# Two edits in a graph network kernel: where VectorE prepares the next pair of tiles, and which engine adds an output bias

## The chip, the cores and the metric

The kernel runs on 1 core of one Trainium2 chip. The metric is device time in microseconds (us) for the whole program; lower is better.

## What the reference computes

The input is a graph of 12,500 nodes with 256 features each and 212,500 weighted edges. Everything is fp32.

```python
xn = _layernorm(x)
x = x + L0_gnn(xn, edges) + L0_mix(xn)       # layer 0: graph convolution, linear attention mixer
x = x + L0_ffn(_layernorm(x))                # layer 0: mixture of 8 experts, two best per token
xn = _layernorm(x)
x = x + L1_gnn(xn, edges) + L1_mix(xn)       # layer 1: graph sum, linear attention block
x = x + L1_ffn(_layernorm(x))                # layer 1: attention over slices

# inside L0_gnn
h = agg + (dinv * dinv)[:, None] * (xn @ W)  # the node's own share beside the sum over its edges
h = 0.5 * _layernorm(h + b) * gamma + ... + 0.5 * xn ; h = relu(h)

# inside L1_ffn, its last line: slice_weights is (12500, 512), slice_out is (512, 256)
return out_x @ W_out + b_out
```

The output is `x` after both layers, 12,500 x 256.

## The kernel before, in words

The program is a sequence of stages. Two of them are touched.

**`finish_layer0`** (span 3143 to 5930 us of the profile) takes what an earlier stage has summed over the edges (`k.sums`, kept in SBUF) and does the rest of layer 0: the product of the graph convolution, the query side of the mixer, the eight experts, and the key side of layer 1's norm. It works on *pairs* of tiles of 125 nodes, `TE` = 2 and `NP` = 50 pairs. Three pairs are in flight at once in one `run(i, n, turn)`: the experts of pair `i` (`moe`), the front of pair `f = i + 1` (`front`) and the back of pair `b = i - 1` (`back`). Each engine has its own copy of `run` with 32 *slots*, written out by hand; the order of the slots is the order of that engine's instructions, and semaphores couple the engines. TensorE issues in slot 0 and 1 the first layer ("up") of expert 0, in slot 2 and 3 the up products of expert 1, then down products and up products in turn (`chunk(slot)`), down products of expert 6 in slots 28 and 29, of expert 7 in slots 30 and 31. Slots 26 and 27 hold only up products of expert 7, so VectorE has no `expert_sum` there.

The pairs run as: two written-out runs (a prologue without experts, and run 0), then a hardware loop `Fori(0, (NP - 2) // 2)` with two runs in its body (runs 1 to 48), then two written-out runs. All engines share this `pipeline`.

What concerns the change, in the order of VectorE's slots:

- slot 0: `back_norm` (L1500, L1504: statistics of the experts' result `acc` of pair b), then four steps of `inverse_root`, then `x_and_sums(0)`; slot 1: four more steps, `x_and_sums(1)`; slot 2: the last four steps; slot 3: `back_rows` (L1562).
- `x_and_sums(j)` (L1570 to L1582): one `tensor_scalar` writes the normalised rows `xn` of pair f (L1576), one `scalar_tensor_tensor` writes `s = xn * dinv + sums` (L1580). It waits for the load of x (`x_in`), for the previous pair's residual chain (`h_chain`), and for the previous transposes (`T_done`).
- slot 4: `expert_sum(0, 0)` (L1543) and `gcn(0)` (L1587), which frees TensorE's PSUM bank `ps_M` for the query product.
- slot 13: `gcn_residual`, the last reader of `xn` and of `x` of pair f; SyncE then loads the x of the next pair (L1425).
- slots 24 and 25: `expert_sum` of expert 5; slot 28: `expert_sum(6, 0)`, then the router's logits (L1673).

TensorE transposes `xn` and `s` of pair f in slots 2 and 3 (`turn_xs`, L1947 and L1948, waits for `xs_ready`), ScalarE copies them out of PSUM (L1799), and TensorE multiplies them in slots 4 to 7 (`gcn`, `query`, both through L1953). TensorE's second-bias product (L1937) of slot 23 waits for VectorE's L1550.

**`write_out`** (span 9330 to 9634 us, the last stage) computes for 50 pairs of tiles x3 + slice weights @ `slice_out` + `b_out`. Per pair SyncE loads the slice weights `sw` and the rows `x3` into one of four buffers, TensorE turns `sw` with 8 transposes (L3120), ScalarE and VectorE copy one tile each out of PSUM (`keep`, L3093), TensorE forms the product of the pair before in `ps_o` (`product`, L3124 to L3131), VectorE adds `x3` to it (L3106), and GpSimd issues the stores (L3084). The product begins with one matmul of a row of ones by the bias (L3125, `start=True`), and 8 matmuls by `slice_out` (L3129) accumulate on top. A matmul of the program shows as two matmuls in the trace.

## Time and profile before

| | us |
|---|---|
| median of 3 runs | 9634.83 (9633.47 to 9641.52) |
| profiled execution, its own time | 9635.69 |
| span of the profiled execution, first to last instruction | 9634.1 |
| TensorE busy | 7447.9 (77%) |
| VectorE busy | 6285.8 (65%) |
| GpSimd busy | 5605.1 (58%) |
| ScalarE busy | 1679.3 (17%) |

The stages follow one another and have different limits, so these shares are only an average. `finish_layer0` fills about 29% of the span and `write_out` about 3%. The time outside the span is 1.6 us.

### The profile page before, as it was taken

What the parts mean: (1) busy time and instruction counts of PE and PEld (TensorE: products, weight loads), DVE (VectorE), ACT (ScalarE), POOL (GpSimd) and SP (SyncE); (2) the same over time, 40 slices, a digit from 0 to 9 for tenths busy, and PEclk for the clock granted to TensorE, in tenths of its full rate; (3) what the DMA queues carried; (4) which work ended last, traced back from release to release, by engine and by line L of the source; (5) the groups of instructions that cost most, each with busy time, mean ns of one, the idle gap of its engine ahead of it and who ended that gap; (6) DMA issues with size and microseconds to landing.
All of it is one profiled execution on the core that took longest, in us unless ns stands there. A gap on an engine that the chain in (4) does not pass through costs nothing. (4 is left out here: it accounts for less than half of the span.)

```text
span 9634.1 us, 141965 instructions
## 1 busy us (share of the span) xinstructions
PE 7447.9 (77%) x34023; PEld 5485.8 (57%) x34023; DVE 6285.8 (65%) x21621; ACT 1679.3 (17%) x3225; POOL 5605.1 (58%) x6034
## 2 busy tenths in 40 slices
PE   4834777677676788888888887788888888877779
PEld 3633555555555566666666665556555565655556
DVE  5746777777777666666666665566666666667742
ACT  0000000000000333433433432111111011112210
POOL 3225777777776555655655655777777777730002
PEclk7657888888888899999999997898898898889989
DMA  1024333333333100000000000333333333333336
GB/s 50 30 74 125 109 107 109 109 107 109 106 110 103 33 16 17 16 15 17 16 16 17 17 15 25 113 107 104 105 105 103 107 104 104 105 86 92 94 96 167
DMA packets 464055, 737.23 MB, mean 77 GB/s; under 512 B 145169, under 2 KB 317487, under 8 KB 463067
## 3 DMA queue, kind: packets, MB, share of 16 engines
q0 software_dynamic: 235408, 493.09, 18.3%
q1 hardware_dynamic: 214944, 224.70, 8.3%
q10 hardware_dynamic: 13240, 15.44, 0.6%
q14 instruction: 437, 3.58, 0.1%
q8 instruction: 26, 0.43, 0.0%
HBM read 624.32 MB, written 108.50 MB: 76 GB/s over the span
## 5 line engine op out<-in xcount | busy, mean ns | idle before, releaser
L894 POOL DMA_INDIRECT sum_gathered<-table,sum_idx x3600 | 3506.2, 974 | 1196.3 <-issue 996.4
L959 PE MATMUL sum_agg_res<-sum_gathered,sum_lay 125*125 125x256 f32 x7200 | 2259.6, 453 | 931.1 <-DMA sum_gathered<-table,sum_idx 346.5
L1463 POOL DMA_INDIRECT sorted_recs<-fin_rec,fin_pos x1700 | 1659.7, 976 | 1147.7 <-PE fin_ps_up L1916 656.8
L959 PEld LDWEIGHTS sum_agg_res<-sum_gathered,sum_lay 125*125 125x125 f32 x7200 | 1466.2, 218 | 1492.2 <-DVE all_sums L944 943.4
L944 DVE TENSOR_TENSOR all_sums<-all_sums,sum_agg_res 125x256 f32 x3600 | 1509.6, 419 | 1050.2 <-PE sum_agg_res L959 842.8
L925 DVE TENSOR_SCALAR sum_lay<-all_lane,sum_dloc_now,sum_w_now 125x125 f32<-125x125 f32 x3612 | 1281.0, 355 | 21.0 <-DVE sum_xn_tiles L1076 16.9
L1916 PE MATMUL fin_ps_up<-fin_tokens_T,fin_w 128*128 128x250 f32 x3200 | 865.2, 397 | 51.4 <-ACT fin_hidden L1791 51.4
L1924 PE MATMUL fin_ps_dn<-fin_w,fin_hidden 128*125 128x256 f32 x3200 | 883.7, 413 | 0.1
L1543 DVE SCALAR_TENSOR_TENSOR fin_acc<-fin_ps_dn,fin_comb,fin_acc 125x256 f32<-125x256 f32 x800 | 386.3, 483 | 562.0 <-PE fin_ps_dn L1924 553.4
L1916 PEld LDWEIGHTS fin_ps_up<-fin_tokens_T,fin_w 128*128 128x128 f32 x3200 | 600.3, 201 | 169.4 <-ACT fin_hidden L1791 86.6
L1924 PEld LDWEIGHTS fin_ps_dn<-fin_w,fin_hidden 128*125 128x125 f32 x3200 | 619.5, 204 | 130.0 <-issue 42.1
L1791 ACT ACTIVATE fin_hidden<-fin_ps_up,fin_b 128x250 f32<-128x250 f32 x800 | 370.4, 469 | 960.4 <-PE fin_ps_up L1916 958.6
L2462 PE MATMUL sum_ps_A<-sum_w,sum_low 128*125 128x256 f32 x1600 | 378.0, 379 | 0.0
L2710 POOL TENSOR_SCALAR slices_var_eps<-slices_mean_var 125x2 f32<-125x2 f32 x50 | 11.0, 219 | 616.2 <-DVE slices_mean_var L2753 604.0
L2453 PE MATMUL sum_ps_C<-sum_x_T,sum_w 128*128 128x500 f32 x800 | 368.4, 582 | 0.0
L2462 PEld LDWEIGHTS sum_ps_A<-sum_w,sum_low 128*125 128x125 f32 x1600 | 300.2, 188 | 116.0 <-issue 80.7
L1059 DVE CUSTOM_DVE_ANT_0 sum_junk<-sum_src_hot,sum_ps_rank 125x100 f32<-125x100 bf16 x1700 | 335.2, 253 | 1.5 <-PE sum_ps_rank L1127 1.5
L2827 PE MATMUL slices_ps_acc<-slices_xn,slices_sw 125*128 125x257 f32 x800 | 229.9, 439 | 121.3 <-DVE slices_sw L2778 121.3
L1049 DVE TENSOR_TENSOR sum_src_hot<-sum_lane,steps_src_tile 125x400 bf16<-125x400 bf16 x425 | 242.9, 571 | 65.6 <-PE sum_ps_rank L1135 58.9
L2385 ACT ACTIVATE sum_low<-sum_ps_C,sum_b 128x500 f32<-128x500 f32 x200 | 135.4, 677 | 722.0 <-PE sum_ps_C L2453 722.0
L1111 ACT ACTIVATE sum_exp_key<-sum_key_less_max 125x256 f32<-125x256 f32 x100 | 41.6, 416 | 1259.2 <-DVE sum_key_less_max L1086 1259.2
L2827 PEld LDWEIGHTS slices_ps_acc<-slices_xn,slices_sw 125*128 125x128 f32 x800 | 165.8, 218 | 166.8 <-DVE slices_sw L2778 142.4
(484 smaller groups left out, 10795.8 us busy)
## 6 DMA issues: line engine op xcount, KB each, us to landing
sum_gathered<-table,sum_idx POOLq DMA_INDIRECT x3600
sorted_recs<-fin_rec,fin_pos POOLq DMA_INDIRECT x1700
slice_weights<-slices_sw SPq DMA_DIRECT2D x50, 480.0 KB
out_sw<-slice_weights SPq DMA_DIRECT2D x50, 480.0 KB
deg_x_tiles<-in_x SPq DMA_DIRECT2D x100, 125.0 KB
sum_x_tiles<-in_x SPq DMA_DIRECT2D x100, 125.0 KB
fin_x<-in_x SPq DMA_DIRECT2D x100, 125.0 KB
x<-fin_acc SPq DMA_DIRECT2D x100, 125.0 KB
```

The lines of the kernel that those rows point to most:

```text
L894: eng.indirect_dma_start(out=self.rows[:, s % self.RING, :], out_offset=None, in_=self.table, in_offset=bass.IndirectOffsetOnAxis(ap=self. ...
L925: ins = eng.tensor_scalar(self.lay[:, g % 2, l, :], k.lane[0:P, 0:P], self.dl[:, s:s + 1], self.wl[:, s:s + 1], ALU.is_equal, ALU.mult)
L944: eng.tensor_tensor(sums, sums, res, ALU.add).then_inc(self.added, 1)
L959: eng.matmul(self.res[s % self.RES][:, 0, :], self.lay[:, g % 2, l, :], self.rows[0:P, s % self.RING, :], start=True, stop=True).then_inc( ...
L1463: eng.indirect_dma_start(out=k.sorted_recs, out_offset=bass.IndirectOffsetOnAxis(ap=pos[:, n, r:r + 1], axis=0), in_=rec[:, n, r, :], in_o ...
L1543: eng.scalar_tensor_tensor(out=acc[:, n, j, :], in0=ps_dn[j][:, :], scalar=comb[:, n, j, e:e + 1], in1=acc[:, n, j, :], op0=ALU.mult, op1= ...
L1791: eng.activation(hid[:, e % 2, c, :], ps_up[c][:, :], ACT.Gelu, bias=b1[:, c, e:e + 1])\
L1916: mm = eng.matmul(ps_up[c][:, :], w1[:, e, m, c * H2:(c + 1) * H2], xtT[:, n, m, :, :], start=(m == 0), stop=(m == 1))
L1924: mm = eng.matmul(ps_dn[j][:, :], hid[:, e % 2, m, j * P:(j + 1) * P], w2[:, e, m, :], start=(m == 0), stop=(m == 1))
L2453: mm = eng.matmul(ps_C[u % 2][:, 0:T], w1[:, m, u * 128:(u + 1) * 128], xT[:, m, :], start=(m == 0), stop=(m == 1))
L2462: mm = eng.matmul(ps_A[j // 2][0:P, (j % 2) * D:(j % 2 + 1) * D], hid[:, u % 2, j * P:(j + 1) * P], w2[:, u, :], start=(u == 0 and j % 2 = ...
L2827: mm = eng.matmul(ps_acc[c][:, :], sw[:, n, j, c * 128:(c + 1) * 128], xn[:, n, j, :], start=False, stop=False, skip_group_check=True)
```

## The change

In `finish_layer0`, VectorE no longer does `x_and_sums` of pair f in slots 0 and 1 of run i. It does it one pair ahead, for pair f + 1, in slots 26 and 27 of run i. The prologue still does pair 0 at its slots 0 and 1 and now also pair 1 in its slots 26 and 27. The last run with a front has nothing to do ahead. VectorE therefore has a `pipeline` of its own, whose loop has one iteration fewer, with two more runs written out. `expert_sum` of expert 0 gets a wait of its own for `comb_ready`.

In `write_out`, the bias is loaded once and broadcast to 125 partitions. VectorE adds it to `x3` in place after its `keep`, and TensorE's ones-by-bias matmul is gone; each group of four products starts its own accumulation.

```diff
-            def run(i, n, turn, front=True, moe=True, back=True):
+            def run(i, n, turn, front=True, moe=True, back=True, ahead=True):
...
                     eng.wait_ge(S.dn_done, at + 1)
                     if e == 0:
                         eng.wait_ge(S.xt_added, i * TE + j + 1)
+                        eng.wait_ge(S.comb_ready, i * TE + j + 1)
...
-                def x_and_sums(j):
-                    t = f * TE + j
-                    eng.wait_ge(x_in[j], f * 16 + 16)
-                    if moe:
-                        eng.wait_ge(S.h_chain, f * 8 - 1 + j)
+                def x_and_sums(p, j):
+                    t = p * TE + j
+                    eng.wait_ge(x_in[j], p * 16 + 16)
+                    if not isinstance(p, int) or p > 0:
+                        eng.wait_ge(S.h_chain, p * 8 - 1 + j)
                         eng.wait_ge(S.T_done, t - 1)
...
-                        if slot < 2:
-                            x_and_sums(slot)
+                        if slot < 2 and not moe:
+                            x_and_sums(f, slot)
+                        elif ahead and 26 <= slot < 28:
+                            x_and_sums(f + 1, slot - 26)
...
-            pipeline(eng, run)
+            run(0, 0, 0, moe=False, back=False)
+            run(0, 0, 0, back=False)
+            with eng.Fori(0, (NP - 4) // 2) as m:
+                run(m * 2 + 1, 1, m)
+                run(m * 2 + 2, 0, m + 1)
+            run(NP - 3, 1, (NP - 4) // 2)
+            run(NP - 2, 0, (NP - 2) // 2, ahead=False)
+            run(NP - 1, (NP - 1) % 2, (NP - 1) // 2, front=False)
+            run(NP, NP % 2, NP // 2, front=False, moe=False)
...
-        bo = sb("b_out", [1, TE, D])
-        ones = sb("ones", [1, P])
+        bo = sb("b_out", [P, D])
...
-            for j in range(TE):
-                eng.dma_start(bo[:, j, :], k.L1_ffn_b_out.rearrange("(a n) -> a n", a=1)).then_inc(b_in, 16)
+            eng.dma_start(bo[:], k.L1_ffn_b_out.rearrange("(a n) -> a n", a=1).to_broadcast([P, D])).then_inc(b_in, 16)
...
         @block.vector
         def _(eng):
+            eng.wait_ge(b_in, 16)
+
             def run(i, n, turn):
                 keep(eng, eng.tensor_copy, i, n, 1)
+                eng.wait_ge(in_[n], turn * 64 + 64)
+                eng.tensor_tensor(x3[:, n, :, :], x3[:, n, :, :], bo[:].unsqueeze(1).to_broadcast([P, TE, D]),
+                                  ALU.add).then_inc(biased, 1)
+                eng.wait_ge(biased, i + 1)
                 eng.wait_ge(done, i + 1)
...
-            eng.wait_ge(b_in, 32)
-            eng.wait_ge(ones_ready, 1)
-
...
-                eng.matmul(ps_o[n][:, :, :], ones[:], bo[:, :, :], start=True, stop=False, skip_group_check=True)
                 for j in range(TE):
                     eng.wait_ge(kept[j], i + 1)
                     for c in range(4):
-                        mm = eng.matmul(ps_o[n][:, j, :], swT[:, n, j, c, :], k.slice_out[:, c, :], start=False,
-                                        stop=False, skip_group_check=True)
+                        mm = eng.matmul(ps_o[n][:, j, :], swT[:, n, j, c, :], k.slice_out[:, c, :], start=(c == 0),
+                                        stop=(c == 3))
```

## Rows read from the trace of the kernel before

**Rows 1.** Windows of loop, `write_out`: length, busy PE/PEld/DVE/ACT/POOL, PEclk, DMA share, GB/s.
```profile
3235.50:5840.10 2604.60, 2230.37 (x9683) 1719.87 (x9682) 1682.79 (x6439) 1029.63 (x2022) 1559.37 (x1599) 0.93 0.07 17
...
9330.00:9634.10 304.10, 282.69 (x1300) 209.46 (x1300) 63.92 (x100) 28.75 (x50) 65.94 (x100) 0.96 0.62 169
```

**Rows 2.** Waits, 3235 to 5840 us: total us, times, longest us.
```profile
PE fin_ps_T L1947 <- DVE fin_sum_self L1580: 137.3, 61, 4.7
...
PE fin_ps_M L1937 <- DVE fin_acc L1550: 107.5, 47, 2.3
...
DVE fin_stats L1500 <- issue: 66.8, 23, 3.1
```

**Rows 3.** Timeline of TensorE at a loop start: start us, duration us.
```profile
4893.40 1.11 PE L1916 MATMUL fin_ps_up<-fin_tokens_T,fin_w 128*128 128x250 f32 x4 [1.07 <-ACT fin_hidden L1791]
4899.02 0.47 PE L1947 MATMUL fin_ps_T<-all_ident,fin_xn 125*128 125x125 f32 x1 [4.51 <-DVE fin_sum_self L1580]
...
4905.40 1.03 PE L1953 MATMUL fin_ps_M<-fin_w_q,fin_xn_sum_T 128*125 128x256 f32 x4
```

**Rows 4.** Timeline of VectorE at the same loop start.
```profile
4895.59 0.75 DVE L1500 BATCH_NORM_STATS2 fin_stats<-fin_acc 125x6 f32<-125x256 f32 x2 [3.00 <-issue]
...
4897.88 0.41 DVE L1576 TENSOR_SCALAR fin_xn<-fin_x,all_mean,all_rstd 125x256 f32<-125x256 f32 x1 [0.30 <-issue]
4898.48 0.48 DVE L1580 SCALAR_TENSOR_TENSOR fin_sum_self<-fin_xn,all_dinv,all_sums 125x256 f32<-125x256 f32 x1 [0.18 <-DVE fin_xn L1576]
...
4901.69 0.74 DVE L1562 TENSOR_SCALAR fin_next_norm<-fin_acc,fin_mean_var,fin_rstds 125x256 f32<-125x256 f32 x2 [0.24 <-DVE fin_rstds L1526]
```

**Rows 5.** Timeline of TensorE in the second run of the loop body.
```profile
4950.99 1.11 PE L1916 MATMUL fin_ps_up<-fin_tokens_T,fin_w 128*128 128x250 f32 x4 [1.07 <-ACT fin_hidden L1791]
4953.42 0.33 PE L1947 MATMUL fin_ps_T<-all_ident,fin_xn 125*128 125x125 f32 x1 [1.31 <-DVE fin_sum_self L1580]
...
4955.24 0.33 PE L1947 MATMUL fin_ps_T<-all_ident,fin_xn 125*128 125x125 f32 x1 [0.32 <-DVE fin_sum_self L1580]
...
4955.72 1.03 PE L1924 MATMUL fin_ps_dn<-fin_w,fin_hidden 128*125 128x256 f32 x4
```

**Rows 6.** Timeline of VectorE: `expert_sum(6, 0)` of slot 28, then next run's `back_rows`.
```profile
4944.29 0.48 DVE L1543 SCALAR_TENSOR_TENSOR fin_acc<-fin_ps_dn,fin_comb,fin_acc 125x256 f32<-125x256 f32 x1 [3.00 <-PE fin_ps_dn L1924]
...
4956.06 0.74 DVE L1562 TENSOR_SCALAR fin_next_norm<-fin_acc,fin_mean_var,fin_rstds 125x256 f32<-125x256 f32 x2 [0.22 <-DVE fin_rstds L1526]
```

**Rows 7.** Timeline of SyncE: the loads of x for the next pair.
```profile
4923.24 0.76 SPq L1425 DMA_DIRECT2D fin_x<-in_x  x2
```

**Rows 8.** Timeline of TensorE after two of its waits for L1550.
```profile
4935.67 0.69 PE L1937 MATMUL fin_ps_M<-fin_b,fin_comb_T 8*125 8x256 f32 x2 [2.28 <-DVE fin_acc L1550]
...
4937.25 3.52 PE L1924 MATMUL fin_ps_dn<-fin_w,fin_hidden 128*125 128x256 f32 x8
...
4970.43 1.99 PE L1924 MATMUL fin_ps_dn<-fin_w,fin_hidden 128*125 128x256 f32 x8
...
4988.53 1.21 PE L1937 MATMUL fin_ps_M<-fin_b,fin_comb_T 8*125 8x256 f32 x2 [2.30 <-DVE fin_acc L1550]
...
4991.50 3.62 PE L1924 MATMUL fin_ps_dn<-fin_w,fin_hidden 128*125 128x256 f32 x8
```

**Rows 9.** Timeline of TensorE and VectorE in `write_out`.
```profile
9354.41 1.02 PE L3120 MATMUL out_ps_T<-all_ident,out_sw 125*128 125x125 f32 x8
...
9355.36 1.12 PE L3125 MATMUL out_ps_o<-out_b_out,out_ones 1*125 1x512 f32 x2
...
9356.41 3.72 PE L3129 MATMUL out_ps_o<-last_slice_out,out_sw_T 128*125 128x256 f32 x16
...
9359.96 1.02 PE L3120 MATMUL out_ps_T<-all_ident,out_sw 125*128 125x125 f32 x8
9360.17 0.69 DVE L3106 TENSOR_TENSOR out_res<-out_ps_o,out_x 125x512 f32<-125x512 f32 x1 [4.28 <-PE out_ps_o L3129]
...
9360.77 0.67 DVE L3093 COPY out_sw_T<-out_ps_T 128x500 f32<-128x500 f32 x1
```

More of the change, by code:

```diff
@@ L3033, in write_out @@
         out_ = [sem(f"out{n}") for n in range(2)]
-        b_in, ones_ready, turned, done, added = (sem(n) for n in ("b_in", "ones_ready", "turned", "done", "added"))
+        b_in, biased, turned, done, added = (sem(n) for n in ("b_in", "biased", "turned", "done", "added"))
         kept = [sem(f"kept{j}") for j in range(TE)]
@@ L3078, in _ @@
         def _(eng):
-            eng.memset(ones[:], 1.0).then_inc(ones_ready, 1)
             def run(i, n, turn):
```

## The prediction

> **What bounds the kernel now.** I read four views in this order.
>
> First the windows [rows 1]. In the loop of `finish_layer0` TensorE is busy 2230 of 2605 us, at a mean granted clock of 0.93. VectorE is busy 1683 us of it, so VectorE has room on average, and what matters is where TensorE waits for it. In `write_out` TensorE is busy 283 of 304 us, and the DMA engines 62%: TensorE sets that stage.
>
> Second the chain of waits in the loop [rows 2]. TensorE's largest wait with a cause in VectorE is the one the change aims at: the transposes of L1947 wait 137.3 us in total for L1580, the end of `x_and_sums`. The second is the second-bias product waiting for L1550, 107.5 us, which the change leaves. VectorE itself starts 23 of its runs 66.8 us late, 2.9 us each, with nothing to wait for ("issue"): these are the 23 jumps back to the head of its loop.
>
> Third the timelines of one loop body, which holds two runs. The loop's window covers 47 runs [rows 1], so a body takes 2 x 2604.6 / 47 = 111 us. At the loop start TensorE ends its up product at 4894.51 and sits idle 4.51 us [rows 3]. VectorE came out of its jump at 4895.59, did the statistics, four root steps, and then the first L1576 and L1580 [rows 4]. In the second run there is no jump, and TensorE waits 1.31 and 0.32 us for the two halves [rows 5]. Check on the total: 23 waits of about 4.5 us are 103 us; the other 38 of the 61 waits share 34 us, 1.4 us for each of 24 pairs.
>
> Last, `write_out`. One pair takes 9359.96 - 9354.41 = 5.55 us, and in it TensorE goes from transposes (0.95 us from start to start) to the bias (1.05) to the products (3.55) without a gap [rows 9].
>
> **`x_and_sums` moved: the second run of the body.** Without the wait, the first transposes start about where the up product's last part is issued, near 4951.95 instead of 4953.42, and the second ones follow the up product between them. The second ones also need ScalarE's copy of the first; that up product (0.9 us) about covers it. I get the first down product at 4953.8 where the trace has it at 4955.72 [rows 5]: 1.9 us saved (1.31 + 0.32, and 0.3 for the restart of a drained TensorE). Does VectorE keep up? Its slots 0 to 3 end with `back_rows` at 4956.06 + 0.74 = 4956.8 [rows 6], and lose 2.3 us of `x_and_sums` (worked out below): 4954.5, before that down product ends at 4954.7. Yes. The term is 24 x 1.9, and the entry run of the loop counts as one more: 25 x 1.9 = 47.5 us.
>
> **`x_and_sums` moved: the loop start.** TensorE now does the two transposes, the up product between, down(0,0), the `gcn` product and down(0,1) from 4894.5 on: two times 0.45 and four times 0.9 (four matmuls of this size take 3.55 / 4 in `write_out` [rows 9]), 4.5 us, so it is done near 4899.0. The query product then waits for `gcn(0)` in VectorE's slot 4. VectorE still leaves its jump at 4895.59. It had finished `back_rows` at 4901.69 + 0.74 = 4902.43. One half of `x_and_sums` costs 0.41 + 0.18 + 0.48 less the overlap with what follows, 1.0 us, and the first has 0.30 of address work ahead [rows 4]: 2.3 us for both, so `back_rows` now ends at 4900.1. `expert_sum(0,0)` and L1587, of L1580's kind and 0.48 each, take 0.9 with overlap: 4901.0, and the query product can start at 4901.2. In the trace it starts at 4905.40 [rows 3]. So 4.2 us are saved up to this point, and a new wait of about 2.2 us appears in front of the query product. What is late next is VectorE's jump itself.
>
> **What the clock gives or takes.** After the 4.51 us idle TensorE ran slow: the first transpose took 0.47 us [rows 3], against 0.33 in the second run [rows 5]. That loss lies before the query product and is inside the 4.2. But the new wait of 2.2 us is as long as the waits for L1550, and behind those the clock falls too [rows 8]: after 2.28 us of idle eight down matmuls took 3.52 us where the same eight take 1.99 elsewhere, a loss of 1.5; after 2.30 us the loss was (4991.50 - 4988.53) - (4937.25 - 4935.67) = 1.4, plus 3.62 - 1.99 = 1.6, so 3.0. These rows are the 1.2 GHz level beside 2.4 GHz. On the other side, in the second run 1.07 and 1.31 us of idle close together brought no slow transposes [rows 5]. The bounds are 0 and 3.0 us per loop start; 2.2 us is nearest to the waits for L1550, and I take a fall of about 2.2 us in two of three, 1.5 us. The term is 23 x (4.2 - 1.5) = 62 us; with the bounds, 28 to 97 us.
>
> A rule speaks about this: the Trainium skill, "TensorE: Matmul & The Clock Gate", section "Part 1: The HAM clock gate", says that the granted clock follows how busy the array has recently been. By that rule, an array that still stalls 2.2 us keeps drawing a fall each time; at 2.2 us a fall this term would be 23 x (4.2 - 2.2) = 46 us instead of 62. The rows agree as to the two waits for L1550 and do not decide for a stall with other neighbours.
>
> **Where the moved work lands.** Before slot 28 VectorE sits idle 3.00 us [rows 6]. The four operations take 2.3 us, so they fit with 0.7 us to spare, and I cost them at nothing. Behind them on VectorE stand `expert_sum(6, 0)` and the logits; TensorE's second router product waits for the logits. If the cover were gone, 2.3 us would fall on every pair, 49 x 2.3 = 113 us. The move issues no DMA. The x it needs is requested after slot 13, at 4923.24 [rows 7], 18 us before slot 26 begins on VectorE (4941.3, where the 3.00 us idle starts). No queue is passed by anything else: SyncE's order stays. The `comb_ready` wait is for VectorE's own work, long done: nothing.
>
> **VectorE's loop.** One of the 23 jumps becomes straight code: up to 2.9 us, and the new wait in that run is gone. The prologue's next pair is prepared in idle time. I take 3 us together; below nothing if the longer program fetches badly, at most one more pause of 3.0 us for each of the two written-out runs, so -6 to +5.
>
> **The bias.** TensorE loses 50 x 1.05 [rows 9]: 53 us, a pair going from 5.55 to 4.50 us. VectorE gains one addition of 0.69 us, priced by L3106, the same shape. It stands between `keep` and the wait for the product. After a product ends, VectorE does L3106, `keep` (to 9361.44, 1.5 us after the product ended) and now the addition, to 2.2 us; the next product ends 4.5 us after. TensorE needs that `keep` 0.95 + 8 x 0.22 = 2.7 us after. So both are covered; without the cover the addition would cost 50 x 0.69 = 35 us. The DMA share of 0.62 becomes at least 0.62 x 5.55 / 4.50 = 0.76, over the whole stage. TensorE waits for a load only at the stage's start. The load of a pair is released two pairs ahead, 11 us before, now 9 us. The broadcast load is one small transfer more in front of the first pair, under 0.5 us. The bounds are 53, and 25 us if transfers hold the pair at 5.0 us.
>
> **The sum.** 47.5 + 62 + 3 + 53 = 165.5 us. From the profiled execution's own 9635.69 (its span is 9634.1) this gives 9470.2; the median is 0.9 us lower, so I say 9470.
>
> **The rivals.**
> *(a) The clock does not fall behind the new wait.* For it: the wait has dense work around it. The loop-start term is 97 and the time 9435. Chance 0.10. *The clock falls every time, at the dearer price*: 23 x 3.0 instead of 23 x 1.5 makes 9505. For it: both waits of 2.3 us drew one [rows 8]. This is where the clock rule named above would lead. Chance 0.08.
> *(b) `write_out` turns to its transfers.* At 0.76 mean share bursts may queue. A pair at 5.0 us gives 28 us less: 9498. Against: the share leaves a quarter free. Chance 0.10.
> *(c) The gain of the second run is absorbed* by the exchange of TensorE, VectorE and ScalarE between slots 4 and 9, each waiting for the other's last result: all 47.5 gone, 9518. Against: those waits are for work that moves forward along with the rest. Chance 0.08.
> *(d) Slower: the moved work is late in slot 26.* If the two halves took more than the 3.00 us there, each us over delays the logits, the router and the next pair. It turns the sign at 165 / 49 = 3.4 us over, 6.4 us for work worked out at 2.3; for 0.2% slower, 3.8 us over. For it: VectorE has only 0.7 us to spare, and the operations wait on three other engines' signals. Time at 4.5 us over: 9690. Chance 0.03.
> *(e) Nothing measurable:* both edits hidden by waits that take their place; 9630. Chance 0.03.
> The forecast holds 0.58, with a range of its own of 9450 to 9490.
>
> **How the numbers follow.** No change means within 0.2%, 19 us, about what a measurement of this kernel can tell. The range 9434 to 9510 takes in the forecast, (a) on both sides and (b), 0.86, and with errors of size at its ends I hold it for 8 in 10. Faster: 0.58 + 0.10 + 0.08 + 0.10 + 0.08 = 0.94; same 0.03; slower 0.03.
>
> **What would show it.** TensorE's wait for L1580 is gone from the loop. At the loop starts a wait of about 2.2 us for L1587 stands before the query product. L1576 and L1580 sit in the 3.00 us idle before slot 28, and the logits are not later behind them. A loop body takes about 106.4 us instead of 111. L3129 recurs every 4.50 us in `write_out`. The prediction is wrong if the jump's 2.9 us grows, if the new wait is far from 2.2 us, if the slow stretches get more, or if transposes in `write_out` begin to wait for loads.

## The result and the profile after

The changed kernel takes 9318.23 us (median of 4 runs, 9310.56 to 9324.18), the kernel before, beside it, 9635.92 (4 runs, 9633.47 to 9641.52). The ratio is 0.9669, 95% interval 0.9652 to 0.9686: faster, by 318 us. The forecast was 9470 us with a range of 9434 to 9510, so the direction was right and the gain about twice what the sum held. The profiled execution took 9324.18 us (span 9322.6).

The stages follow one another, so each can be read in the trace, from the end of the stage ahead of it to its own last record. What lies ahead of the first stage of the table (624 us) and between the two layers (81 us) is the same in both kernels within 1 us.

| stage, us | before | after | difference | forecast |
|---|---|---|---|---|
| sums over edges, layer 0 | 2488 | 2489 | +1 | 0 |
| `finish_layer0` | 2835 | 2648 | -187 | -112.5 |
| sums over edges, layer 1 | 2527 | 2469 | **-58** | 0 |
| slices | 776 | 771 | -5 | 0 |
| `write_out` | 305 | 242 | -63 | -53 |

`write_out` came near its term. `finish_layer0` gave 75 us too much, and 58 us come from a stage that the change leaves alone. The 5 us of the slices do not come back when both kernels are run again (their last part takes 43 us in three of the four profiles and 39 in this one), so they are chance.

The windows of the changed kernel (columns as in [rows 1]): the loop of `finish_layer0`, `write_out`, and the steady part of `write_out`.

```profile
3276.00:5650.00 2374.00, 2104.65 (x9500) 1622.54 (x9498) 1642.08 (x6309) 1010.49 (x1983) 1534.21 (x1568) 0.98 0.08 18
9081.00:9322.60 241.60, 219.06 (x1200) 192.88 (x1200) 93.82 (x150) 28.76 (x50) 65.95 (x100) 0.95 0.77 213
9115.00:9296.00 181.00, 181.00 (x1009) 160.06 (x1008) 78.74 (x126) 24.16 (x42) 55.25 (x84) 1.00 0.86 238
```

In the loop TensorE's clock is 0.98 where it was 0.93 [rows 1]; this is the first hint at the 75 us. In `write_out` TensorE is busy all 181 of 181 us in the steady part, with the DMA engines at 0.86, so TensorE still sets the pace and the transfers do not.

The waits of the changed kernel in `finish_layer0`, 3240 to 5650 us (columns as in [rows 2]):

```profile
PE fin_ps_M L1948 <- DVE fin_acc L1551: 107.3, 47, 2.3
...
PE fin_ps_M L1964 <- DVE fin_gcn L1588: 37.9, 22, 2.3
...
DVE fin_stats L1500 <- issue: 65.1, 22, 3.4
```

TensorE's wait for the end of `x_and_sums`, 137.3 us in [rows 2], is gone. In its place stands a wait for `gcn` (now L1588) at the 22 loop starts, 1.7 us each (37.9 / 22). The jump of VectorE's loop costs as before, and the wait for the second bias still is 107 us.

A loop start on TensorE, timeline of the changed kernel:

```profile
4676.56 1.11 PE L1927 MATMUL fin_ps_up<-fin_tokens_T,fin_w 128*128 128x250 f32 x4 [1.07 <-ACT fin_hidden L1802]
4677.51 0.27 PE L1958 MATMUL fin_ps_T<-all_ident,fin_xn 125*128 125x125 f32 x1
...
4681.13 1.03 PE L1935 MATMUL fin_ps_dn<-fin_w,fin_hidden 128*125 128x256 f32 x4
4684.08 1.13 PE L1964 MATMUL fin_ps_M<-fin_w_q,fin_xn_sum_T 128*125 128x256 f32 x4 [1.92 <-DVE fin_gcn L1588]
4685.04 1.01 PE L1927 MATMUL fin_ps_up<-fin_tokens_T,fin_w 128*128 128x250 f32 x4
```

The order of work is the forecast's: transposes at once (0.27 us where [rows 3] has 0.47 after 4.51 us of idle), four blocks of products, then a wait of 1.92 us in front of the query product. But the up product right behind the query product takes 1.01 us, full speed. The clock does not fall here. The next two groups show the second-bias wait of two runs in the same trace:

```profile
4661.20 0.69 PE L1948 MATMUL fin_ps_M<-fin_b,fin_comb_T 8*125 8x256 f32 x2 [2.28 <-DVE fin_acc L1551]
4661.82 1.77 PE L1927 MATMUL fin_ps_up<-fin_tokens_T,fin_w 128*128 128x250 f32 x4
4663.38 2.96 PE L1935 MATMUL fin_ps_dn<-fin_w,fin_hidden 128*125 128x256 f32 x8
```

```profile
4714.56 0.69 PE L1948 MATMUL fin_ps_M<-fin_b,fin_comb_T 8*125 8x256 f32 x2 [2.30 <-DVE fin_acc L1551]
4715.18 1.11 PE L1927 MATMUL fin_ps_up<-fin_tokens_T,fin_w 128*128 128x250 f32 x4
4716.13 1.89 PE L1935 MATMUL fin_ps_dn<-fin_w,fin_hidden 128*125 128x256 f32 x8
```

The same wait, 2.28 and 2.30 us, drew the lower level (1.2 GHz) once, with eight down products in 2.96 us, and not the other time, 1.89. Both waits in [rows 8] drew it. Over the whole loop the records of granted clock show 355 us at the lower level before and 113 after, although this wait itself is as long as before. Sorted by the last wait of TensorE of over 1.2 us that had begun when the clock fell:

| last long wait begun before the fall | before: waits, falls, us at the lower level | after: waits, falls, us |
|---|---|---|
| transposes for L1580, at a loop start (4.4 us) | 23, 23, 157 | gone |
| transposes for L1580, second run (1.3 us) | 19, 6, 20 | gone |
| second bias for L1550, now L1551 (2.3 us) | 47, 46, 177 | 47, 28, 106 |
| query product for `gcn`, at a loop start (1.7 us) | none | 22, 2, 7 |

So a fall behind the new wait is the exception: 2 of 22 here, and 5 of 22 when the changed kernel was run again. And the waits for L1551 draw fewer falls than the same waits did before.

VectorE in slots 26 to 28, timeline of the changed kernel:

```profile
4718.50 0.41 DVE L1577 TENSOR_SCALAR fin_xn<-fin_x,all_mean,all_rstd 125x256 f32<-125x256 f32 x1
4719.09 0.49 DVE L1581 SCALAR_TENSOR_TENSOR fin_sum_self<-fin_xn,all_dinv,all_sums 125x256 f32<-125x256 f32 x1 [0.18 <-DVE fin_xn L1577]
...
4721.49 0.48 DVE L1544 SCALAR_TENSOR_TENSOR fin_acc<-fin_ps_dn,fin_comb,fin_acc 125x256 f32<-125x256 f32 x1 [0.93 <-PE fin_ps_dn L1935]
```

The moved work starts at 4718.50 and leaves 0.93 of the 3.00 us of idle in [rows 6]. It is hidden, as forecast.

A body of the loop, cut at TensorE's records, in us. Each part is the mean over the 22 or 23 turns of the loop's window in which all records of the cuts are there:

| part of a loop body | before | after | difference | forecast |
|---|---|---|---|---|
| loop start: last up product ahead of the transposes to query product | 11.99 | 7.31 | -4.7 | -4.2 |
| second run: the same | 7.78 | 5.43 | -2.4 | -1.9 |
| query product to second-bias wait, both runs | 55.93 | 56.23 | +0.3 | +1.5 |
| the second-bias wait, both runs | 4.58 | 4.57 | 0 | 0 |
| its end to the next run's last up product, both runs | 30.75 | 29.53 | -1.2 | 0 |
| body | 111.0 | 103.1 | -8.0 | -4.6 |

`write_out`, timeline of TensorE and VectorE in the changed kernel:

```profile
9106.76 1.02 PE L3130 MATMUL out_ps_T<-all_ident,out_sw 125*128 125x125 f32 x8
...
9107.62 3.62 PE L3138 MATMUL out_ps_o<-last_slice_out,out_sw_T 128*125 128x256 f32 x16
...
9108.21 0.68 DVE L3113 TENSOR_TENSOR out_x<-out_x,out_b_out 125x512 f32<-125x512 f32 x1
...
9111.07 1.02 PE L3130 MATMUL out_ps_T<-all_ident,out_sw 125*128 125x125 f32 x8
```

A pair takes 9111.07 - 9106.76 = 4.31 us, not 4.50. The transposes take 0.86 us from start to start where they took 0.95 beside the bias product, the products 9111.07 - 9107.62 = 3.45 where they took 3.55 [rows 9]. VectorE's addition lies in the middle of the products and nobody waits for it.

### The profile page after: what moved, and what is told of

The parts are those of the page before. It is cut to its first block and busy times, and to the rows that moved or that the text cites. A ratio compares the mean times of both kernels' runs of the same rounds, so it can differ in the third digit from the quotient of the medians.

```text
span 9322.6 us, 141852 instructions
## 1 busy us (share of the span) xinstructions
PE 7264.5 (78%) x33923; PEld 5393.6 (58%) x33923; DVE 6311.5 (68%) x21671; ACT 1679.3 (18%) x3225; POOL 5603.3 (60%) x6033
## 5 line engine op out<-in xcount | busy, mean ns | idle before, releaser
L944 DVE TENSOR_TENSOR all_sums<-all_sums,sum_agg_res 125x256 f32 x3600 | 1510.0, 419 | 1008.1 <-PE sum_agg_res L959 839.6
L1927 PE MATMUL fin_ps_up<-fin_tokens_T,fin_w 128*128 128x250 f32 x3200 | 838.7, 388 | 51.4 <-ACT fin_hidden L1802 51.4
L1935 PE MATMUL fin_ps_dn<-fin_w,fin_hidden 128*125 128x256 f32 x3200 | 847.8, 400 | 0.1
L1935 PEld LDWEIGHTS fin_ps_dn<-fin_w,fin_hidden 128*125 128x125 f32 x3200 | 595.5, 196 | 123.2 <-issue 43.0
```

The costliest lines, as they stand in the source:

```text
L944: eng.tensor_tensor(sums, sums, res, ALU.add).then_inc(self.added, 1)
L1927: mm = eng.matmul(ps_up[c][:, :], w1[:, e, m, c * H2:(c + 1) * H2], xtT[:, n, m, :, :], start=(m == 0), stop=(m == 1))
L1935: mm = eng.matmul(ps_dn[j][:, :], hid[:, e % 2, m, j * P:(j + 1) * P], w2[:, e, m, :], start=(m == 0), stop=(m == 1))
```

## The experiments

The chips did not all run the kernel before at one level: the first measurement and two later sets took about 9640 us, three other sets 11,319, 11,490 and 11,321 us (below called the longer level, of times and not of the clock). Each kernel is compared with the kernel before on its own chip; the last part of this section tells what the longer level is. The sets at 9640 us come first, since they decide.

### The change again, and the kernel before again

Both kernels unaltered. `before_look` is one profiled execution.

> The changed kernel itself, unaltered, on the chip of these runs. If the gain of the moved step belongs to the kernel, it is about 3.3% faster again than the kernel before beside it. If the gain of the first layer shows only where the kernel before takes 9636 us, and this chip is one on which it takes about 11,400, the ratio is that of the bias part alone, 0.994 to 0.996; the run with four products of filling gave 0.990, which leaves room for a gain of 30 to 50 us from the rest.

> The kernel before, for its trace on the chip of these runs. If this chip is like the one of the two calls ahead, the three stages with indirect transfers take about 3,150, 3,400 and 3,050 us in place of 2,488, 2,835 and 2,527, and the stages without them stay within 5 us; the wait of TensorE's transposes for the addition of the sums (L1580) is then partly replaced by pauses that name no releaser. If the chip is like that of the first measurement, it takes 9,636 us.

Measured: 9330.58 us against 9640.66, ratio 0.9677 (0.9661 to 0.9693). Stages: `finish_layer0` 2657 against 2840, layer 1's sums 2454 against 2528, `write_out` 244 against 305. The result repeats, the 58 us in untouched code too (74 here). Two profiles of one kernel differ by 5 to 9 us in `finish_layer0` and by up to 15 in layer 1's sums (2469 and 2454 for the changed kernel); that is how far single stages can be trusted below.

### Is it the idle time or the clock?

Products that add zero are put in TensorE's queue where it would idle. Every wait of the work itself stays. The four products stand in every run, so twice in a loop body (the expectations say "in each body"); the eight ahead of the transposes at a loop start (the last two lines) are in the kernel before alone.

```diff
+                def fill(count):
+                    for _ in range(count):
+                        eng.matmul(ps_ctx[0][:, :], w1[:, 0, 0, 0:128], flat[:, :], start=False, stop=False,
+                                   skip_group_check=True)
                 def second_bias(j):
                     if j == 1:
+                        fill(4)
...
+                    elif moe and n == 1:
+                        fill(8)
```

> The kernel before with products that add zero put in TensorE's queue where it waits: eight ahead of the transposes at each loop start, four ahead of the second bias in each body. No wait is taken away; TensorE only works while it waits. If most of the 187 us of the first layer's last stage came from the clock (355 us at the lower level before, 113 after, so about 120 us of lost work), this kernel's stage is 80 to 150 us shorter than the 2,835 us of before, and few stretches at the lower level are left. If the gain was the idle time itself, the stage stays within 20 us, or is longer by the products.

> The changed kernel with four such products ahead of the second bias in each body. If the clock's falls that are left in it stand behind that wait (113 us at the lower level, half of it lost work), it is 30 to 60 us faster than the 9,320 of the changed kernel: 9,265 to 9,290. If those falls come from elsewhere it stays within 10 us of 9,320.

`fill_before` took 9524.23 us against 9637.6, ratio 0.9892 (0.9875 to 0.9908): 113 us faster with more work on TensorE. `fill_good`, the changed kernel with the four products, took 9281.99, ratio 0.9637 (0.9621 to 0.9654). Both are as expected. In `fill_good` the 27 us left at the lower level all stand behind the wait for `gcn`, which drew a fall in 8 of 22 turns. The loop's window, first of `before_look`, then of `fill_before`, then of `fill_good`:

```profile
3240.00:5840.00 2600.00, 2227.93 (x9646) 1717.69 (x9645) 1673.86 (x6399) 1026.21 (x2013) 1552.20 (x1592) 0.93 0.07 17
```

```profile
3240.00:5720.00 2480.00, 2258.75 (x10405) 1758.78 (x10403) 1678.25 (x6403) 1027.65 (x2016) 1559.66 (x1591) 1.00 0.08 17
```

```profile
3240.00:5600.00 2360.00, 2166.47 (x9976) 1682.76 (x9976) 1656.57 (x6387) 1021.80 (x2007) 1546.30 (x1584) 0.99 0.08 18
```

With 759 more matmul records in the window TensorE is busy for only 31 us more, and the clock is 1.00. Two of TensorE's waits in `fill_before`, same window:

```profile
PE fin_ps_T L1957 <- DVE fin_sum_self L1582: 66.9, 86, 1.7
...
PE fin_ps_M L1945 <- DVE fin_acc L1552: 26.3, 47, 0.6
```

What TensorE waits for did not go away; the products fill most of the time, and shorter waits are left (those for the sums are more in number, 86, since TensorE arrives sooner). The four runs make a square of `finish_layer0`, in us, with the time at the lower level summed from the records of granted clock, without the long stretches at the stage's two ends. The filled kernels ran on another chip than the two beside them; there the unfilled kernel before takes 2835 and 2839 us in this stage (`unroll_good` and `pad64`, below).

| | as it is | filled | clock's share |
|---|---|---|---|
| step not moved (`before_look`, `fill_before`) | 2840, lower level 369 | 2718, lower level 27 | 122 |
| step moved (`after_again`, `fill_good`) | 2657, lower level 137 | 2605, lower level 31 | 52 |
| what the move gives | 183 | 113 | 70 |

So of 183 us, about 113 are idle time taken away, which remain when the clock is held up in both kernels, and about 70 are the clock, falling less, each good to some 10 us. Where the clock's 70 lie, the parts of a body tell. Filled, the part behind the second-bias waits takes 27.3 us in both kernels; unfilled it takes 30.8 before and 29.5 after. The falls there cost 3.5 us a body before and 2.2 after, a gain of about 30 us over the stage. The other 40 or so are slow stretches up to the query product, at the loop start above all (11.99 us there become 10.67 with filling).

### Is it a transfer that makes the difference?

GpSimd's 17 indirect transfers a pair are replaced by one plain transfer; the second layer then sums over other edges, so its values are others. `flat_move` has the moved step too, the bias as before.

```diff
-                    for r in range(group * RPP // NE, (group + 1) * RPP // NE):
-                        eng.indirect_dma_start(
-                            out=k.sorted_recs, out_offset=bass.IndirectOffsetOnAxis(ap=pos[:, n, r:r + 1], axis=0),
-                            in_=rec[:, n, r, :], in_offset=None).then_inc(scattered[n], 16)
+                    if group == 0:
+                        eng.dma_start(flat_recs[:, bass.ds(i * RPP, RPP), :], rec[0:P, n, :, :]).then_inc(scattered[n], 16)
...
```

> The kernel before, in which the first layer's last stage writes the edge records with one plain transfer a pair, in place of 17 indirect ones from GpSimd (the second layer then sums over other edges, so its numbers are others). If the indirect transfers make the first layer's last stage longer where the kernel before takes 11,400 us, that stage falls from about 3,400 to about 2,800 us here, and the pauses of VectorE, ScalarE and TensorE without a releaser go. If they have nothing to do with it, the stage stays within 50 us of the unaltered kernel's.

> The same with the moved step in it (norm of x and addition of the sums one pair ahead), and with the bias as before. If the move's gain was hidden under the pauses that the indirect transfers bring, this kernel is 110 to 190 us faster than the one with plain transfers and without the move. If the pauses come from elsewhere, the two lie within 30 us of one another. If the gain of the move came itself from the way the scatters fall among the slots, it is gone in this pair wherever it runs.

Measured: 9626.72 us (ratio 0.9984, 0.9975 to 0.9994) and 9379.73 (0.9723, 0.9707 to 0.9739). `finish_layer0` takes 2823 and 2647 us, layer 1's sums 2522 and 2462. The move gives 247 us here, 176 in its own stage and 60 in layer 1's sums. The gain of the move stays without the indirect transfers of this stage (176 us beside 183 and 187), so they have no measurable part in it. As this set ran at the 9640 us level, it says nothing of whether they make the longer level.

### Where do the 58 us in untouched code come from?

`unroll_good` is the kernel before with VectorE's loop written out as in the change and nothing moved. `pad64`, `pad8` and `pad360` put empty instructions right behind VectorE's loop of `finish_layer0`, so ahead of its code for layer 1 (the expectations call this place "ahead of the loop", which holds for layer 1's loop alone).

```diff
-            pipeline(eng, run)
+            run(0, 0, 0, moe=False, back=False)
+            run(0, 0, 0, back=False)
+            with eng.Fori(0, (NP - 4) // 2) as m:
+                run(m * 2 + 1, 1, m)
+                run(m * 2 + 2, 0, m + 1)
...
```

The padded kernels, in place of that:

```diff
             pipeline(eng, run)
+            for _ in range(64):
+                eng.nop(nofuse=True)
```

> The kernel before with VectorE's loop written out as in the change, and nothing moved. If the 58 us of the second layer's sums, whose code the change leaves alone, come from where VectorE's later code stands, that stage falls from 2,527 to about 2,465 us here and the whole to about 9,575. If they come from the moved step itself (another state of memory or of the transfers when the second layer starts), the kernel stays at 9,635.

> The kernel before with 64 empty instructions ahead of VectorE's loop in the first layer's last stage; the code of everything behind stands 64 instructions later. If the second layer's sums depend on where VectorE's loop begins, their stage moves off 2,527 us by tens of us in one or the other direction. If the difference comes from how much code lies behind or from the loop's own form, it stays within 5 us, and the kernel takes 9,636.

> The kernel before with 8 empty instructions where the last run had 64. With the loop written out, VectorE's pause ahead of its first addition behind the jump of the second layer's loop is 0.88 us; in the kernel before it is 2.54 us and with 64 empty instructions 2.58. If the pause depends on the loop's place within a small block of code, in which 16 and 64 instructions are whole blocks, 8 put it elsewhere: the pause changes by more than 0.3 us and the second layer's sums by more than 15 us. If it depends on the amount of code, or on something else that writing out the loop changes, nothing moves: 2.5 us and 9,636 us.

> The same with 360 empty instructions, about as many as writing out the loop adds ahead of the second layer's loop (360 records in the trace). If distance alone matters, the pause falls to about 0.9 us and the second layer's sums from 2,527 to about 2,470 us, less up to 20 us for issuing the empty instructions once. If it is the place within a block of 16 or fewer, nothing is certain: 360 is a multiple of 8 and not of 16, so pad8 and pad360 should then show the same pause. If both show 2.5 us, the cause is neither, and stays open.

`unroll_good` took 9562.76 us against 9637.6, ratio 0.9924 (0.9907 to 0.9940). In its profile layer 1's sums take 2474 us (2528 in `before_look`) and `finish_layer0` 2835: nothing from the first layer, 54 us from the stage in question. (The profiled execution, 9590 us, was the slowest of its four; about 22 us of the median's gain stand in no trace.) `pad64` took 9636.68, ratio 1.0001 (0.9991 to 1.0011), the stage 2518: 10 us less in this profile and nothing in the time, neither the "tens of us" of its expectation nor within its 5.

VectorE behind the jump of layer 1's loop, first in `before_look`, then in `unroll_good`:

```profile
6949.53 0.34 DVE L914 CAST sum_dloc_now<-steps_dloc_p 125x78 f32 x1 [2.76 <-issue]
6949.66 0.26 DVE L915 COPY sum_w_now<-steps_w_p 125x78 f32 x1
6950.05 0.37 DVE L925 TENSOR_SCALAR sum_lay<-all_lane,sum_dloc_now,sum_w_now 125x125 f32<-125x125 f32 x1
6952.96 0.42 DVE L944 TENSOR_TENSOR all_sums<-all_sums,sum_agg_res 125x256 f32 x1 [2.54 <-issue]
```

```profile
6942.74 0.35 DVE L925 TENSOR_SCALAR sum_lay<-all_lane,sum_dloc_now,sum_w_now 125x125 f32<-125x125 f32 x1
6943.97 0.42 DVE L944 TENSOR_TENSOR all_sums<-all_sums,sum_agg_res 125x256 f32 x1 [0.88 <-issue]
```

Behind the jump there is a second pause with nothing to wait for, 2.54 us before and 0.88 with the loop written out, in front of the same addition. Such pauses recur through the loop's turns. Over the whole stage the idle time before L944 that waits for nothing falls from 126.5 us to 91.2, 35 of the 54 us; between the first two profiles it falls from 125.7 to 86.0, 40 of the 58. The rest of the 54 and 58 us is not accounted for. `pad64` and, on another chip, `pad360`:

```profile
6952.72 0.42 DVE L944 TENSOR_TENSOR all_sums<-all_sums,sum_agg_res 125x256 f32 x1 [2.58 <-issue]
```

```profile
7633.14 0.42 DVE L944 TENSOR_TENSOR all_sums<-all_sums,sum_agg_res 125x256 f32 x1 [2.77 <-issue]
```

Moving the code by 64 or by 360 instructions leaves the pause. Over the stage the same idle time is 115.6 us with 64 and, at the longer level, 142.8 with 360 and 126.1 with 8. The times of `pad8` (11,349.32 us, ratio 1.0015, 0.9995 to 1.0034) and `pad360` (11,323.26, 0.9993, 0.9971 to 1.0015) are those of the kernel before, within an interval that is too wide at that level to rule out a gain of 30 us. More code alone, in these four amounts, does not shorten the pause. But `fill_before`, whose VectorE program has a single instruction more ahead of this loop (the `memset` of the zeros), shows the pause elsewhere:

```profile
6936.68 0.20 DVE L915 COPY sum_w_now<-steps_w_p 125x78 f32 x1
6938.76 0.41 DVE L925 TENSOR_SCALAR sum_lay<-all_lane,sum_dloc_now,sum_w_now 125x125 f32<-125x125 f32 x1 [1.88 <-issue]
6939.97 0.42 DVE L944 TENSOR_TENSOR all_sums<-all_sums,sum_agg_res 125x256 f32 x1 [0.80 <-issue]
```

Here it is split, 1.88 and 0.80 us, and the stage takes 2525 us: no gain, another place. In `fill_good`, which has the same instruction more and the written-out loop, nothing is split and the idle time before L944 is 87.4 us, as without it (83.3 and 86.0). That would fit a pause set by where the code lies within a block of eight instructions or fewer, which all four paddings (8, 16, 64, 360) leave as it is and one instruction does not. No run moved the code by 2 to 7 instructions, so this stays an argument, and why the written-out loop shortens the pause stays open. Shown is: the 58 us come with the written-out loop, not with the moved step, and 8, 16, 64 or 360 instructions of padding do not bring them.

### The sets at the longer level

> The kernel before with the new write_out alone; VectorE's program ahead of that stage is untouched. Prediction's term: 53 us less, from 50 ones-by-bias products at 1.05 us. Reading of the changed kernel's trace: the recurrence of one pair fell from 5.55 to 4.31 us, so about 61 us less; the surplus of 0.19 us a pair is time that the neighbours of the bias product lost. Rival (the transfers took over in write_out): 25 us or less. In every theory finish_layer0 and the layer-1 aggregation keep their lengths (L1916 ends near 5926 us, L944 near 8545 us).

> The changed kernel with the old write_out: x_and_sums one pair ahead, VectorE's loop written out by one body. If the two edits are independent and write_out is worth 61 us, this is 317 - 61 = 256 us faster than before, of it 188 us in finish_layer0 and 57 us in the layer-1 aggregation, whose code is not touched. By the prediction's sum it would be 112 us. If the 57 us in the layer-1 stage hang on the new write_out, this is under 210 us faster.

> The kernel before, VectorE's loop in finish_layer0 one iteration shorter and two more runs written out, x_and_sums where it was. Nothing moves but the place of VectorE's later code. Theory A (the place of the layer-1 loop's head in VectorE's program sets its pauses for code): the pause of about 1.5 us at the 8th record behind the jump changes or goes, and the layer-1 stage is some 40 to 57 us shorter. Theory B (the layer-1 gain comes from the work of finish_layer0 ending otherwise, its buffers or its transfers): layer-1 stage unchanged within 5 us. Both: finish_layer0 unchanged within 6 us.

> The kernel before with 16 empty instructions on VectorE behind its last run in finish_layer0, executed once (about 1 us). Theory A: the head of the layer-1 loop stands 16 instructions later, the early pause behind its jump goes, and 40 to 57 us are saved with no other edit. Theory B: nothing is saved, 0 to 2 us are lost.

> Second run of the kernel with only the move and VectorE's own loop. On a chip where the kernel before takes about 9636 us as in its own trace: 256 us faster (188 in finish_layer0, 57 in the layer-1 aggregation) if the trace of the changed kernel adds up. On a chip where it takes 11319 us again, no change, as in the first run.

> Second run of the kernel with VectorE's loop written out by one body and nothing moved. Where the kernel before takes about 9636 us: theory A (place of the layer-1 loop in VectorE's program) 40 to 60 us faster, all of it in the layer-1 aggregation; theory B 0.

> Second run of the kernel with 16 empty instructions on VectorE behind finish_layer0. Where the kernel before takes about 9636 us: theory A 40 to 57 us faster, the pause at the 8th record behind the layer-1 loop's jump gone; theory B 0 to 2 us slower.

> The changed kernel, with four products by a tile of zeros added into a bank of the context sums (they add nothing) in front of TensorE's wait for L1550, the 2.3 us stall that the change left. They take 1.7 us at full clock, so they end inside the stall. If what is left of the slow stretches comes from that stall (113 us of slow clock in the loop in the changed trace, 30 stretches), they go and the kernel gains 30 to 50 us over the changed one. Rival (VectorE sets the pace behind that stall, the clock costs nothing there): within 5 us of the changed kernel.

`bias_only` has `write_out` of the changed kernel, `move_only` the rest of the change, `pad16` is a padding as above, `fill_after` is the same kernel as `fill_good`; "again" is a second set with the same kernels.

| kernel | before beside it | this | ratio (95% interval) | `finish_layer0` | layer 1's sums | `write_out` |
|---|---|---|---|---|---|---|
| bias_only | 11,319.08 | 11,273.32 | 0.9962 (0.9942 to 0.9982) | 3363 | 3064 | 243 |
| move_only | 11,319.08 | 11,335.39 | 1.0013 (0.9991 to 1.0034) | 3386 | 3020 | 305 |
| unroll_only | 11,319.08 | 11,291.25 | 0.9974 (0.9957 to 0.9990) | 3360 | 2994 | 306 |
| pad16 | 11,319.08 | 11,327.74 | 1.0003 (0.9979 to 1.0027) | 3330 | 3040 | 304 |
| move_again | 11,489.71 | 11,486.78 | 1.0012 (0.9990 to 1.0034) | 3486 | 3035 | 304 |
| unroll_again | 11,489.71 | 11,462.60 | 0.9987 (0.9966 to 1.0007) | 3435 | 3031 | 305 |
| pad16_again | 11,489.71 | 11,479.47 | 1.0010 (0.9991 to 1.0029) | 3431 | 3064 | 304 |
| fill_after | 11,489.71 | 11,354.19 | 0.9897 (0.9865 to 0.9929) | 3417 | 3010 | 243 |

Three things follow. The bias part gives its 62 us (305 to 243) at either level. The written-out loop shortens the idle time before L944 here too, to 98.8 and 90.3 us from 153.7 and 131.3 in the padded kernels, and the stage by 46 and 33 us (stages scatter by tens of us at this level, though: `pad8` and `pad360`, on one chip and both with the pause, take 3071 and 3015), while 16 instructions of padding bring none of the 40 to 57 us that theory A of the expectations wanted. And the move gives nothing that can be told from no change here, 3386 and 3486 us beside 3330 and 3431 for the padded kernel, where it gave 183 at the other level; `move_only`, expected 256 us faster, was not. The changed kernel as it stands was not run at this level, only with filling. Only the three stages in which GpSimd issues indirect transfers are longer, by 17 to 31%; slices and `write_out` agree within a few us. Largest waits of VectorE in `pad16`, 3300 to 5900 us:

```profile
DVE fin_acc L1543 <- PE fin_ps_dn L1926: 458.1, 266, 6.1
DVE fin_acc L1543 <- remote: 99.8, 39, 5.3
```

In `before_look` no wait of VectorE has "remote" as its releaser in that stretch, and the longest wait for the down product is 3.4 us, not 6.1. Pauses of up to 5 or 6 us fall on VectorE, ScalarE and TensorE at many places of these stages. A saving of 2 to 5 us at a loop start may vanish in such a pause, which no run shows; these sets tell only that the move was worth nothing measurable here. What makes the pauses was not found: the kernel with plain transfers, which was to tell, ran at the 9640 us level.

## Why the prediction was wrong

**Right.** The bound of each stage, the disappearance of the wait for L1580, the place and nearly the size of the new wait (1.7 us, forecast as 2.2), the cover of the moved work in slot 26, no transfer problem in `write_out` at a DMA share of 0.86 (rival (b), which the forecast gave 0.10), the unchanged price of the jump.

**The step that failed: "What the clock gives or takes".** It subtracted 1.5 us at each of 23 loop starts for a fall of the clock behind the new wait, 34.5 us. The runs show 2 falls behind 22 such waits (5 of 22 in the second profile), and 0.3 us in place of 1.5. It took the wait's length as what decides, and the two waits of 2.3 us above show that the same length can cost nothing. It was right that the slow stretch behind the 4.51 us wait lies before the query product and is inside the 4.2 us. But it never asked what the vanished waits do to the falls behind L1550, in the same loop body: that term was put at nothing and measured 1.2 us a body, about 30 us (46 falls became 28). Both errors have the same sign, 1.2 us a body each. Why the same wait draws fewer falls in the changed kernel (the waits missing around it, or the shorter body) no run separates.

Rival (a) had the first of the two, no fall behind the new wait, with a chance of 0.10 and a time of 9435 us; it too had nothing for the falls behind L1550, and is 117 us off. The rival with a dearer fall each time, for which the forecast named both waits of [rows 8], went the wrong way.

**Two savings, mis-sized a little.** The loop start gave 4.7 us where the sum had 4.2, the second run 2.4 where it had 1.9, together about 1 us a body. The parts of a body so give 8.0 us where the forecast had 4.6; 3.4 us by 24 bodies are 80 us, the stage's 75 within what single profiles can tell.

**A hit that would have been luck.** Without any fall the sum had 47.5 + 97 + 3 = 147.5 us, of which part is slow clock at the loop starts; less 34.5 it had 113. Filled against filled, the move gives 113 us too. These are not the same 113 us, and that they agree is chance.

**The rule named there.** The Trainium skill, "TensorE: Matmul & The Clock Gate", section "Part 1: The HAM clock gate", says that the granted clock follows how busy the array has recently been. The runs agree, with PEclk from 0.93 to 1.00 and 113 us less time once the waits are filled. The forecast read from it a fall behind every stall of 2.2 us, and the falls behind 2 of 22 such waits do not bear that out. It used the rule only against the change, and here it speaks mostly for it: with 137 us of waits gone for 38 new ones TensorE is busy for 0.89 of the loop's window where it was 0.86.

**A term that was not there.** The sum has no term for layer 1. 58 us came from it, 40 of them idle time of VectorE that waits for nothing and that the written-out loop shortened. The same written-out loop gave `finish_layer0` nothing (2835 us in `unroll_good`), where the sum had 3 us. The prediction did bound what a longer program may do to fetching in `finish_layer0` ("-6 to +5"), but not in the stages whose code stands behind.

**The bias, slightly small.** 50 x (5.55 - 4.31) = 62 us for 53: taking the ones-by-bias product out also shortened its neighbours, 0.09 us at the transposes and 0.10 at the products, 50 x 0.19 = 9.5 us. The bound for transfers that hold a pair at 5.0 us has a slip: such a pair saves 50 x 0.55 = 27.5 us and falls 25 short of the term, so the bound is 28 (it says 25), and the rival's time 9495 (it says 9498). Nothing hangs on it.

The sum that would have been right: 187 us in `finish_layer0` (by the square about 113 idle time and 70 clock), 58 with the written-out loop, 63 in `write_out`, 308 of the 311.5 us between the two spans; the rest is the chance of single profiles.

## What to carry to other kernels

When a change takes stalls away from TensorE, price the clock in both directions: read PEclk in the window, and count how many waits of each kind drew a slow stretch, over the whole stage and not in one or two rows, for every stall of that stage and not only for the one that is moved. To tell idle time from clock, fill the wait with products that add zero; if the kernel gets faster with more work, it was the clock, and the fill is itself an edit worth trying (9282 us here, against 9318 and 9331 for the change without it; the ratios are 0.9637 against 0.9669 and 0.9677, from different chips, and the first two intervals just overlap). Look at all stages after an edit that adds or removes instructions on an engine: a loop that nobody touched can gain tens of us, as layer 1's sums did here.

## What the runs showed of the hardware that was not expected

- A wait of 2.3 us on TensorE may or may not draw the lower clock (eight products in 2.96 or in 1.89 us behind waits of 2.28 and 2.30). With the other stalls of the same loop body gone, the falls behind this wait went from 46 to 28 in 47 runs, and their cost from 3.5 to 2.2 us a body. In the whole stage the clock's share went from 122 to 52 us.
- VectorE pauses twice at the head of a loop: 2.76 us at the jump and, a few instructions on, 0.88 or 2.54 us, with nothing to wait for. One instruction more in the program split and moved the second pause in the kernel before, and did nothing in the changed one; 8, 16, 64 or 360 left it.
- Three of six sets met a level of 11,300 to 11,500 us, where only the stages with indirect transfers are longer, by 17 to 31%, with pauses of several us on the engines. The changed kernel with filling stands at 0.9637 at the one level and at 0.9897 at the other.
- A one-row bias product of 1.05 us between other products cost 1.24 us in all.
